# Two attention stages of a four-layer kernel with their steps written in another order

## The reference

```python
x = x + tanh(g_xattn[0]) * L0_xattn(ctx_1024, layernorm(x), ...)   # first attention, 8 heads of 64
x = x + tanh(g_ffn[0])   * L0_ffn(layernorm(x), ...)
x = x + tanh(g_xattn[1]) * L1_xattn(ctx_1024, layernorm(x), ...)   # 16-head attention, heads of 8
...
# L0_xattn: queries from the latents ln = LN(LN(x)); keys and values from LN(ctx) and from ln,
#   keys of ctx rotated (x*cos + swapped_halves*sin);  softmax(q k^T / 8) over 128 keys;  heads @ Wo
# L1_xattn: s = LN(ctx), t = LN(LN(x)); q = t Wq, k = s Wk, v = s Wv; softmax(q k^T / sqrt(8)) over 64 keys; heads @ Wfc
```

## Time and profile before

| | us |
|---|---|
| median of three runs | 2255.52 (2255.41 to 2260.2) |
| the profiled execution | 2251.0 |
| its span | 2249.2 |
| TensorE busy | 1963.3 (87%) |
| VectorE busy | 1717.3 (76%) |
| ScalarE busy | 1195.4 (53%) |
| granted TensorE clock, mean | 0.945 |

### The profile page before, as it was taken

The page is one execution under the profiler, slowest core; times in us unless marked ns, Lnnn a source line. Parts: engine busy times, 40 slices in busy tenths (PEclk is TensorE's granted clock), DMA queues, the critical chain, the costliest instruction groups (busy, mean ns, idle before and its releaser), DMA issues. The chain is left out here.

```text
span 2249.2 us, 48289 instructions
## 1 busy us (share of the span) xinstructions
PE 1963.3 (87%) x18173; PEld 1508.3 (67%) x18173; DVE 1717.3 (76%) x4753; ACT 1195.4 (53%) x2324; POOL 262.8 (12%) x553
## 2 busy tenths in 40 slices
PE   3999999999986998999989886999999986499808
PEld 2788788888776996777757665577777765244308
DVE  2788888888876987999967786666676668787894
ACT  1565555655553216888856553544454445316844
POOL 0101111011101101111111142000000022200000
PEclk9999999999997999999989997999999999699958
DMA  6221112221113551111100011212211111001452
GB/s 183 50 51 49 47 49 51 51 50 47 47 36 152 227 227 30 30 31 33 30 8 1 10 48 53 80 76 95 95 76 76 76 43 34 0 1 71 173 205 75
DMA packets 123591, 155.71 MB, mean 69 GB/s; under 512 B 47561, under 2 KB 104290, under 8 KB 119266
## 3 DMA queue, kind: packets, MB, share of 16 engines
q1 hardware_dynamic: 117368, 149.92, 20.5%
q10 hardware_dynamic: 5994, 2.70, 0.4%
HBM read 110.11 MB, written 25.69 MB: 60 GB/s over the span
## 5 line engine op out<-in xcount | busy, mean ns | idle before, releaser
L1717 DVE TENSOR_TENSOR arena<-arena 128x512 f32<-128x512 f32 (+1 forms) x256 | 171.1, 686 | 69.6 <-ACT arena L1755 66.3
L1755 ACT ACTIVATE arena<-banks,b1c 128x512 f32<-128x512 f32 x192 | 131.7, 687 | 171.3 <-PE banks L1630 171.1
L1640 PEld LDWEIGHTS banks<-w2a,arena 128*128 128x128 f32 x1024 | 124.1, 192 | 28.7 <-issue 28.7
L885 PE MATMUL banks<-we,arena 128*128 128x128 f32 x1024 | 129.9, 281 | 3.0
L498 PE MATMUL banks<-arena,wk 128*128 128x128 f32 x1024 | 126.7, 278 | 1.1 <-DVE arena L606 1.1
L885 PEld LDWEIGHTS banks<-we,arena 128*128 128x128 f32 x1024 | 120.9, 193 | 9.9 <-DVE arena L949 9.2
L539 PE MATMUL banks<-wv,arena 128*128 128x512 f32 x256 | 125.0, 611 | 2.6 <-ACT arena L652 2.6
L1640 PE MATMUL banks<-w2a,arena 128*128 128x128 f32 x1024 | 124.7, 275 | 0.0
L1630 PE MATMUL banks<-arena,w1s 128*128 128x512 f32 x256 | 122.4, 612 | 0.0
L498 PEld LDWEIGHTS banks<-arena,wk 128*128 128x128 f32 x1024 | 121.0, 194 | 1.7 <-DVE arena L606 1.5
L633 ACT ACTIVATE arena<-banks 128x512 f32<-128x512 f32 x64 | 38.2, 597 | 144.0 <-PE banks L490 144.0
(11 more groups left out here) (271 smaller groups left out, 5061.2 us busy)
## 6 DMA issues: line engine op xcount, KB each, us to landing
arena<-coef_scratch SPq DMA_DIRECT2D x32, 2048.0 KB, 7.0
arena<-arena SPq DMA_DIRECT2D x256, 64.0 KB, 2.0
gated_scratch<-arena SPq DMA_DIRECT2D x16, 768.0 KB, 3.2
arena<-gated_scratch SPq DMA_DIRECT2D x16, 768.0 KB, 4.2
arena<-z1T_scratch SPq DMA_DIRECT2D x128, 64.0 KB, 2.2
arena<-ctxT_scratch SPq DMA_DIRECT2D x32, 256.0 KB, 2.8
arena<-in_ctx SPq DMA_DIRECT2D x64, 64.0 KB, 2.0
z1T_scratch<-arena SPq DMA_DIRECT2D x64, 64.0 KB, 1.7
```

The lines of the kernel that those rows point to most:

```text
L885: mm = pe.matmul(ps[:, OUT + g.par, j * D:(j + 1) * D], xs[g.par][:, n, j * P:(j + 1) * P], k.we0[:, n, :], start=n == 0, stop=n == EXPERT ...
L1640: mm = pe.matmul(ps[:, OUT + g.par, j * D:(j + 1) * D], hT[g.par][:, c, j * P:(j + 1) * P], w, start=c == 0, stop=c == CHUNKS2 - 1)
L1717: dve.tensor_tensor(hT[g.par][rows, c, :], hT[g.par][rows, c, :], wide_coef[g.par][rows, e, :], ALU.mult).then_inc(s["scaled"].sem, 1)
L1755: act.activation(hT[g.par][:, c, :], ps[:, HID + c % NHID, :], ACT.Gelu, bias=k.b1c[:, c:c + 1])\
```

## The change

In the first attention the values are projected for tile s (not s+1) right behind the keys; turned weights follow, then the queries, the turning of the heads of tile s-1, the front of tile s+2, AV of tile s, and last the output of tile s-1. VectorE normalises the heads of tile s at the step's end (not those of tile s-1 at its start), finishes the rotation before it makes Z, and updates x last. ScalarE copies values, turned weights, queries, heads and context in that order. In the 16-head attention the turning of heads (now of tile s-2) and of xhat (now of tile s+1) stands right behind the scores, and the output of tile s-2 moves behind the keys; ScalarE copies those two first in its step. `...` marks what is left out.

```diff
@@ first attention, TensorE
-            if t := at(-1):
-                pe.wait_ge(*s["onorm"](t))
...
-                mm.then_inc(s["ot_psum"].sem, 1)
             if t := at(1):
                 pe.wait_ge(*s["z_ready"](t))
...
                     mm.then_inc(s["k_psum"].sem, 1)
+            if t := at(0):
+                if at(1):
+                    pe.wait_ge(*s["z_ready"](at(1)))
+                    pe.wait_ge(*s["ctxT_sb"](at(1)))
+                if at(-2):
+                    pe.wait_ge(*f["x_updated"](at(-2)))
+                for b in range(PAIR):
+                    mm = pe.matmul(ps[:, 4 + b, :], Z[t.par][:, b].rearrange("p s i -> p (s i)"), k.wv0[:, :],
+                                   start=True, stop=True)
+                    mm.then_inc(s["v_psum"].sem, 1)
+            if t := at(0):
...
+                    mm.then_inc(s["pt_psum"].sem, 1)
+            if t := at(1):
                 if t.has(2):
                     pe.wait_ge(*s["onorm"](t.back(2)))
...
                 mm.then_inc(s["q_psum"].sem, 1)
+            if t := at(-1):
+                pe.wait_ge(*s["onorm"](t))
+                if at(0):
+                    pe.wait_ge(*s["v_sb"](at(0)))
+                elif t.has(1):
+                    pe.wait_ge(*f["x_updated"](t.back(1)))
+                for c in range(HPAIRS):
+                    mm = pe.transpose(ps[:, 5, c * P:(c + 1) * P], on[:, c * P:(c + 1) * P], k.ident)
+                mm.then_inc(s["ot_psum"].sem, 1)
@@ 16-head attention, TensorE, behind the scores
+            if t := at(-2):
+                pe.wait_ge(*s["onorm"](t))
+                if t.has(1):
+                    pe.wait_ge(*f["x_updated"](t.back(1)))
+                pe.transpose(ps[:, 0, 0:D], on, k.ident).then_inc(s["ot_psum"].sem, 1)
+            if t := at(1):
+                pe.wait_ge(*f["xhat_ready"](t))
+                if t.has(3):
+                    pe.wait_ge(*s["onorm"](t.back(3)))
+                pe.transpose(ps[:, 7, 3 * D:4 * D], k.xh[:, t.par, :], k.ident).then_inc(f["xT_psum"].sem, 1)
@@ 16-head attention, ScalarE, first in the step
+            if t := at(-2):
+                act.wait_ge(*s["ot_psum"](t))
+                act.activation(oT, ps[:, 0, 0:D], ACT.Copy).then_inc(s["ot_sb"].sem, 1)
+            if t := at(1):
+                act.wait_ge(*f["xT_psum"](t))
+                act.activation(zt[t.par], ps[:, 7, 3 * D:4 * D], ACT.Identity, scale=k.aff[:, 6:7],
+                               bias=k.aff[:, 7:8]).then_inc(s["zt"].sem, 1)
```

## The result

The changed kernel takes 2243.18 us, the median of seven runs (2234.39 to 2247.44), beside 2255.52 for the kernel before on the same chip: 0.9939 of its time, 95% interval 0.9924 to 0.9954. It is faster by 0.6% by that ratio, some 14 us, and by 12.3 us between the two medians, where 25 were forecast (2230.5). The profiled execution took 2245.9 us, its span 2244.1.

A forecast was written before the change was run, and what follows sets the result against it. TensorE was busy nearly throughout both attentions, but with stalls and mode-change drains in its steps. Savings of 8 us (first attention) and 17 us (16-head) sum to -25, from 2255.5 to 2230.5 us; range 2214 to 2250.

The forecast's parts named there:

- The sign: Whole kernel: the change makes it faster, chance 0.84; same 0.07, slower 0.09.
- First attention, the usual step: First attention: a step falls from 9.64 to 9.52 us, -8 us over 64 steps.
- two limits: First attention: the queries' copy before AV and VectorE's chain behind the swapped keys both give a step of about 9.52 us.
- 16-head attention, the usual step: 16-head attention: a step falls from 4.56 to 4.29 us, by a two-step loop of 8.58 through ScalarE; -17 us.
- the waits foretold: 16-head attention: VectorE's wait on scores nearly gone; TensorE waits, if at all, for ScalarE's copy before turning the second half.
- Late landings: Both attentions: transfers landing late cost nothing in the forecast; 16-head landings from 2.7 us on cost 0.1 per 0.1.
- a general delay of the 16-head loads: Rival, 16-head attention: loads come late, at 3.0 us landing that part's gain is gone; 2247.5 us, chance 0.09.
- a general delay of the swap: Rival, first attention: swap transfers taking 1.4 us more make the step 10.2; 2275 us, chance 0.09.
- Slower behind the swapped keys: First attention, same rival: VectorE's work after the swap wait shifts with the landing, half of any delay entering the step.
- Drain and first step: First attention: the last tile costs about +1 us, the first step starts about 1 us sooner; taken as nothing.
- Time in other stages: Unedited stages: no time should move there; if it did, the prediction called itself wrong.

The follow-up runs named there:

- The early loads: Changed kernel with the 16-head context loads issued one step earlier into three buffers: 2231.89 us, 0.9908; again 2228.60 us, 0.9888.
- both further edits: Changed kernel with 16-head loads a step earlier in three buffers and first-attention statistics taken before the swapped-keys wait: 2231.14, 2222.09, 2224.39 us.
- the early queries: On top of both further edits, first-attention queries projected right behind the keys and copied ahead of the values: 2218.46 us, 0.9855.
- its partner: The version with both further edits, without the early queries, run beside it on the same chip: 2224.39 us, 0.9876.

## Why the prediction was right, and where it was off

The sign, and the range (2214 to 2250), held; the size did not. By its steps:

- **First attention, the usual step.** The prediction took "9.52, **-8 us**". The step is 9.52 in every profile of the new order. The starts in it were right within 0.11 us (the values' is the worst, 2.92 for 2.81). That two limits meet there fits what was seen: shortening VectorE's chain alone leaves the usual step at 9.52, and moving the queries as well gives their place to the turned weights, at 9.54. In the changed kernel's usual step the queries' copy ends at 309.57, 0.11 before AV's first load, and the row before AV says only "issue"; in a step behind a late landing it names that copy:

```profile
358.17 1.15 PE L546 MATMUL banks<-arena 128*64 128x65 f32 x32 [0.21 <-ACT arena L657]
```

- **16-head attention, the usual step.** Forecast 4.29, two steps 8.58; measured 8.54. Right, and so were the waits foretold: TensorE waits 0.21 for ScalarE's copy before it turns the second half (L1071), and VectorE's wait on the scores, 24.7 us in all before its maxima, is down to 2.4.
- **Late landings.** This is the step that failed. They were costed at nothing in the forecast and put into two rivals, a general delay of the 16-head loads and a general delay of the swap. Neither came as a general delay: the swap's median landing is 2.0 us before and after, and the loads' is 2.2 and 2.4. It came as single late ones, up to 3.9 and 4.1 us. The prediction had read this off the median ("Against: the median is 2.2") although its own rows 6 gave 3.4 as the longest, 0.7 over the 2.7 from which on it had itself said that each 0.1 costs 0.1. In the term of the sum: -17 for the 16-head part measured -7 and -16 in two profiles of the changed kernel and -9 in one of this part alone (first to last scores; the three in order against 288.7, 289.0 and 288.7), and -8 for the first attention measured -1 and -4 (610.0 and 609.8). The early loads give the 16-head part its 18 us (270.5).
- **Slower behind the swapped keys.** The mechanism acted, at a small size. "All work after that wait ... now shifts with the landing" is what the 2.40 and 2.51 rows show; the extra of the first attention grew from 2.7 to 9.0 and 5.9 us. But a late landing doesn't cost half of itself, as for a lasting delay: two late ones, of 0.9 and 1.0 us, made the next two steps 1.84 us longer together, nearly all of it.
- **Drain and first step.** Costed at +1 and -1. From the last scores to the last update of x (its start) it is 10.9 us before and 11.9 after, as forecast; the first scores begin 0.8 us sooner (51.12 for 51.94).
- **Time in other stages.** "I am wrong ... if the time moves in a stage that isn't edited." It moved by up to 7 us, in the kernel before as well. Such a move in one pair of profiles says nothing about the change, and the sum had to be checked stage by stage, with more than one profile.

## What to carry to other kernels

When an order is tightened until a step ends as soon as its data is there, look at the longest landing of each transfer, not the median: the slack before its reader must cover the longest one, or each late one passes into the time. Restore the slack where it is cheap, with one more buffer on the load or with independent work ahead of the wait; on the loose order the same edit bought nothing (0.9999), on the tight one it took the ratio from 0.9939 to 0.9908 and 0.9888. And compare stages, not sums: one pair of profiles put 4.5 us on a stage that nobody had edited and that varies by 7.

The version with both further edits and the early queries, 2218.46 us or 0.9855 (0.9838 to 0.9871), has the lowest median of all that ran, ahead of the changed kernel's 0.9939 and of the kernel before; its interval overlaps that of the version without the early queries.

## What the runs showed of the hardware

Transfers of the same size and place land at different times: in the changed kernel the swaps of 64 KB in 1.9 to 3.9 us (median 2.0), the context loads in 2.1 to 4.1 (median 2.4); in the kernel before, up to 3.4 both. The late ones go with fetches of instructions over the same engines. The DMA view of a late 16-head step (988 to 993.5 us, changed kernel), and of the one before it, whose loads landed in time (984 to 988.2):

```profile
q1 hardware_dynamic: 544, 0.13, 11.3%
q8 instruction: 1, 0.02, 1.7%
issues: line engine op xcount, KB each, median us to landing
arena<-z1T_scratch SPq DMA_DIRECT2D x2, 64.0 KB, 3.9
```

```profile
q1 hardware_dynamic: 544, 0.13, 13.8%
issues: line engine op xcount, KB each, median us to landing
arena<-z1T_scratch SPq DMA_DIRECT2D x2, 64.0 KB, 2.3
```

The same view of the steps of the changed kernel, a stretch of 4 us (16-head, from 2.6 after the scores) or 5 us (first attention, from 2.5) that holds the issues and landings, sorted by whether an instruction packet fell into it (steps with a median landing over 2.5 or 2.0 us, of all that show one):

| | with an instruction packet | without |
|---|---|---|
| 16-head loads, over 2.5 us | 22 of 37 | 0 of 24 |
| first attention's swap, over 2.0 us | 8 of 17 | 0 of 45 |

No late transfer without one. The kernel before has the same: 14 of its swaps in the first attention took over 2.4 us (17 in the changed kernel) and 3 of its context loads over 2.7 (28), and an instruction packet ran during each of them. And in the version with the early queries, whose late swaps were gone, an instruction packet ran during 19 swaps, in its partner during 60; 3 and 33 of them were late. That goes together; that the fetch delays the transfer was not tested by a run, since none took the fetches away. It would explain why the late steps of the first attention come some fifteen steps apart, and perhaps, if the phase of the fetches against the steps differs between executions, why the 16-head steps have 12 us of them in one and 4 in the next.

At the changes between full-array and tiled work the next group of matmuls begins 0.07 us before the modelled end of the last one, as the prediction took it (scores to keys, AV to output and output to scores in the step above), where without a change it begins 0.16 or 0.17 before (keys to values, turned weights to queries). Between weight loads the profile shows a gap before AV (0.22 us) and before the keys (0.17) and names no releaser. Such a gap alone is no sign of a change: 0.24 stands between the loads of the values too.
